# The first transfers, folds and sums of an autocorrelation and expert kernel on other queues and engines

## The reference, cut to what matters

```python
def _autocorrelation(Q, K, V):           # per batch, 8 heads, L = 512 positions
    qf = jnp.fft.fft(q, axis=2)
    kf = jnp.fft.fft(k, axis=2)
    corr = jnp.fft.ifft(qf * jnp.conj(kf), axis=2).real
    topk = int(C * np.log(L))            # 12
    w, idx = jax.lax.top_k(corr.transpose(0, 1, 3, 2), topk)
    w = jax.nn.softmax(w, axis=-1)
    for i in range(topk):
        g = jnp.minimum(idx[:, :, None, :, i] + pos, L - 1)
        out = out + w[:, :, None, :, i] * jnp.take_along_axis(v, g, axis=2)

x = x + jnp.tanh(g_xattn[0]) * _L0_xattn_ref(_layernorm(x), ctx_4096, ctx_4096)
x = x + jnp.tanh(g_ffn[0]) * _L0_ffn_ref(_layernorm(x), W_base, b_base, W_gate, W_thr, b_thr, A_w, B_w)
```

## Time and profile before

| | us |
|---|---|
| median of 3 runs | 3143.74 |
| lowest and highest | 3143.69 and 3145.4 |
| the profiled execution's own time | 3146.76 |
| its span, first to last instruction | 3145.0 |
| TensorE busy | 2976.3 (95%) |
| VectorE, GpSimd, ScalarE busy | 1699.9, 1494.1, 861.7 |

### The profile page before, as it was taken

How to read it: one execution, slowest core, us unless ns; L and a number is a source line. 1 busy time by engine, 2 the same in 40 slices (tenths; PEclk the granted TensorE clock), 3 DMA queues, 4 the chain that set the end, 5 groups by cost and what they waited for, 6 DMA issues and landing times.

```text
span 3145.0 us, 35465 instructions
## 1 busy us (share of the span) xinstructions
PE 2976.3 (95%) x12496; PEld 1510.2 (48%) x12496; DVE 1699.9 (54%) x2863; ACT 861.7 (27%) x1253; POOL 1494.1 (48%) x582
## 2 busy tenths in 40 slices
PE   4999999999999999999579999999999999999999
PEld 2545544554545455454354444444444444444444
DVE  4899999999999999988561121121121121121111
ACT  3343334334333433432251111121121121111110
POOL 4878887887888788886212211211211212212210
PEclk8999999999999999999799999999999999999999
DMA  9445544544454455341363232232232232232330
GB/s 213 120 117 127 133 105 120 133 115 113 124 140 101 119 132 119 86 99 49 134 228 86 76 107 82 78 107 78 82 107 75 85 107 72 88 107 67 93 94 28
DMA packets 268310, 333.59 MB, mean 106 GB/s; under 512 B 167321, under 2 KB 167449, under 8 KB 253497
## 3 DMA queue, kind: packets, MB, share of 16 engines
q1 hardware_dynamic: 268226, 332.68, 39.1%
HBM read 231.94 MB, written 67.11 MB: 95 GB/s over the span
## 4 chain that ended last, share of the span: by engine, by line
PE 46%; DVE 3%; DMA 1%; issue 1%; ACT 0%; POOL 0%; DVEq 0%; ACTq 0%; SPq 0%
PE bank L939 42%; DVE row L1094 2%; PE bank L928 1%; PE bank L929 1%; PE bank L930 1%; PE bank L919 1%; DMA row<-in_L_ffn_W_base_dram 1%; DMA row<-in_L_ffn_A_w_dram 0%; PE bank L956 0%; PE bank L954 0%; PE bank L955 0%; DVE w_lo L1033 0%; DMA nt<-wrow 0%; POOL wrow L1120 0%; PE bank L947 0%
## 5 line engine op out<-in xcount | busy, mean ns | idle before, releaser
L1120 POOL TENSOR_TENSOR wrow<-norm,wrow 128x2048 f16<-128x2048 f32 x32 | 130.3, 4071 | 1230.2 <-ACT wrow L992 1230.2
L720 POOL TENSOR_TENSOR spec_o<-spec_o,term 128x1024 f32<-128x1024 f32 x256 | 594.7, 2358 | 31.2 <-DVE term L558 31.2
L939 PE MATMUL bank<-w_hi,wrow 128*128 128x512 f16 x2048 | 489.3, 379 | 3.8 <-DVE row L1094 3.8
L939 PE MATMUL bank<-w_hi,nt 128*128 128x512 f16 x2048 | 489.0, 379 | 3.5 <-DVE row L1094 3.5
L381 PE MATMUL bank<-wt,table 128*128 128x512 f32 x1024 | 450.8, 598 | 25.8 <-DVE prod_b L535 19.0
L1087 DVE TENSOR_TENSOR hwt_lo<-bank,hwt_hi 128x128 f16<-128x128 f32 x32 | 9.3, 292 | 789.9 <-ACT hwt_hi L1011 789.9
L939 PEld LDWEIGHTS bank<-w_hi,wrow 128*128 128x128 f16 x2048 | 200.2, 98 | 251.7 <-DVE row L1094 13.7
L939 PEld LDWEIGHTS bank<-w_hi,nt 128*128 128x128 f16 x2048 | 200.6, 98 | 250.3 <-DVE row L1094 12.7
L381 PEld LDWEIGHTS bank<-wt,table 128*128 128x128 f32 x1024 | 193.1, 191 | 264.6 <-issue 235.7
L939 PE MATMUL bank<-w_lo,wrow 128*128 128x512 f16 x1024 | 262.8, 379 | 0.0
L939 PE MATMUL bank<-w_lo,nt 128*128 128x512 f16 x1024 | 262.8, 379 | 0.0
(11 more groups left out here) (153 smaller groups left out, 4449.4 us busy)
## 6 DMA issues: line engine op xcount, KB each, us to landing
xt<-in_x_dram SPq DMA_DIRECT2D x32, 1024.0 KB, 12.4
norm<-x_scratch SPq DMA_DIRECT2D x32, 1024.0 KB, 5.6
row<-x_scratch SPq DMA_DIRECT2D x32, 1024.0 KB, 7.0
out_dram<-row SPq DMA_DIRECT2D x32, 1024.0 KB, 4.4
xstat<-in_x_dram SPq DMA_DIRECT2D x28, 1024.0 KB, 10.5
vt<-in_ctx_dram SPq DMA_DIRECT2D x256, 64.0 KB
vt<-in_ctx_dram SPq DMA_DIRECT2D x64, 256.0 KB
xres<-in_x_dram SPq DMA_DIRECT2D x256, 64.0 KB
```

Source lines behind the costliest of these rows:

```text
L720: pool.tensor_tensor(to, to, term[:, buffer], sign).then_inc(term_added, 1)
L939: mm = pe.matmul(dense[o][:, :], nt(par, part)[:, k, :], w[:, k, o * 512:(o + 1) * 512], start=(k == 0 and n == 0), stop=False)
L1120: pool.tensor_tensor(norm_lo, norm[:, :], norm_hi, ALU.subtract).then_inc(norm_lo_made, 1)
```

## The change

It has five parts, all ahead of or in the first step. The first two chunks of x are loaded ahead of everything else. The ten transfers of the first v are issued by ScalarE instead of SP. The table is loaded in four parts, two of which (for v and for q) are awaited before the first spectra and two later. The first chunk of x is not loaded a second time into xt: the first normalisation reads it from the buffer prod_a. The first folds of q and the first sums are made by VectorE instead of GpSimd.

```diff
-                load_v(0)
-                load_v_last(0)
-                sp.dma_start(table[:, :], tables[:, 0:I_AT]).then_inc(table_loaded, 16)
                 for n in range(NCH):
-                    sp.dma_start(early[n], x_t[0, :, :, n * C:(n + 1) * C]).then_inc(early_loaded[n], 16)
-                load_x(0)
+                    load_early(n)
+                    if n == 1:
+                        load_v_last(0)
+                        load_table(V_AT, P_AT, first_tables_loaded)
+                        load_table(Q_AT, W_AT, first_tables_loaded)
+                load_table(W_AT, V_AT, table_loaded)
+                load_table(P_AT, I_AT, table_loaded)
...
-                pe.wait_ge(table_loaded, 16)
+                pe.wait_ge(first_tables_loaded, 32)
                 v_spectra(0, X(0))
                 pe.wait_ge(ident_loaded, 16)
+                pe.wait_ge(table_loaded, 32)
...
                 def normalise(i):
-                    act.wait_ge(x_loaded, 16 * (i + 1))
+                    if least(i) >= 1:
+                        act.wait_ge(x_loaded, 16 * i)
                     act.wait_ge(ln1_ready, i // NCH + 1)
                     for t in range(TT):
-                        act.activation(xt[:, t, :], xt[:, t, :], ACT.Identity, bias=ln1_bias[:, t:t + 1],
+                        act.activation(xt[:, t, :], (xt if least(i) >= 1 else early[0])[:, t, :], ACT.Identity, bias=ln1_bias[:, t:t + 1],
...
+                for n in range(8):
+                    act.dma_start(vt[16 * n:16 * n + 16, 0:2, :], v_after[0, 7 - n, :, :, 0:C]).then_inc(v_loaded, 16)
+                for h in range(2):
+                    act.dma_start(vt[:, 2 + h, :], v_before[0, :, :, h, 0:C]).then_inc(v_loaded, 16)
                 act.wait_ge(ei_scale_set, 2)
...
+                def first_fold():
+                    dve.wait_ge(x_normed, 4)
+                    dve.tensor_tensor(qf[:, 0:2, :], xt[:, 0:2, :], xt[:, 2:4, :], ALU.add).then_inc(q_folded, 1)
+                    dve.tensor_tensor(qf[:, 2:4, :], xt[:, 0:2, :], xt[:, 2:4, :], ALU.subtract).then_inc(q_folded, 1)
+
+                def first_sums():
+                    dve.wait_ge(q_used, 2)
+                    dve.tensor_tensor(prod_a[:, 0:2, :], prod_a[:, 0:2, :], prod_b[:, 0:2, :], ALU.add).then_inc(prod_made, 1)
+                    dve.tensor_tensor(prod_a[:, 2:4, :], prod_a[:, 2:4, :], prod_b[:, 2:4, :], ALU.subtract)\
+                       .then_inc(prod_made, 1)
...
                 scales(0)
+                first_fold()
                 dve.wait_ge(gates_ready, 2)
...
                 join_v(0)
-                fold_q(0)
                 fold_v(1)
...
-                    if most(i) < STEPS:
+                    if least(i) >= 1 and most(i) < STEPS:
                         sum_qk(i)
```

More of the change, by code:

```diff
@@ L168, in flamingo_kernel @@
             early = [prod_a[:, :, :], halves[:, :, :], corr[:, :, :], wt[:, :, :]]
-            table_loaded = sem("table_loaded")
+            table_loaded, first_tables_loaded = sem("table_loaded"), sem("first_tables_loaded")
             ei_scale_set = sem("ei_scale_set")
@@ L244, in load_x, with load_table, load_early @@
                     sp.dma_start(xt[:, :, :], x_t[b, :, :, ds(c, C)]).then_inc(x_loaded, 16)
+                def load_table(first, last, loaded):
+                    sp.dma_start(table[:, first:last], tables[:, first:last]).then_inc(loaded, 16)
+                def load_early(n):
+                    sp.dma_start(early[n], x_t[0, :, :, n * C:(n + 1) * C]).then_inc(early_loaded[n], 16)
                 def load_res(i, par):
@@ L652, in step @@
                         q_times_k(i, par, mine)
+                    if most(i) == 0:
+                        first_sums()
                     if least(i) >= 1:
```

## The result

| | before | changed |
|---|---|---|
| median, us | 3144.57 (6 runs beside the change) | 3158.7 (6 runs) |
| lowest and highest | 3142.57 and 3146.84 | 3154.37 and 3159.48 |
| the profiled execution | 3146.76 | 3158.3 |
| its span | 3145.0 | 3156.5 |

The ratio is 1.0041, 95% interval 1.0028 to 1.0054: slower, by 14.1 us between the medians and 11.5 between the two profiled spans. The forecast was 3141.2, a gain, with a chance of 0.02 for a loss of this size.

A forecast was written before the change was run, and what follows sets the result against it. TensorE bounds the loop, so only the prologue chain, with v's and x's chains equally long, could shift: 0.5 + 0 + 1.0 + 1.0 = 2.5 us off the 3145.0 span, 3142.5, by offset 3141.2; range 3134.5 to 3145.0.

The forecast's parts named there:

- I take 13.4, 1.0 later than now, near the lower end because of the idle share: Prologue: first v on ScalarE's queue lands at 13.4 us, as x fits into half idle DMA; root 0.6 us later.
- upper bound of 18.0: Latest landing of the first v, if two x loads (2.1 MB at 385 GB/s, 5.4 us) all go first.
- the second v at 34.0: Prologue: v of chunk 1 lands near 34.0 us instead of about 40.4; GpSimd folds it 34.0 to 38.7.
- the rule of two inputs: A VectorE instruction with two SBUF inputs and a GpSimd instruction reading SBUF share a port pair; the second fully blocks.
- First folds on VectorE, gain 0.5: Folds of q take 2.3 us for 4.65, but VectorE waits for GpSimd until 38.7; end 41.0 against 41.50.
- rival A: VectorE is free of GpSimd: 2.3 us for folds, 2.3 for sums, more in step 1; 8 us, 3135.5; chance 0.2.
- First sums, gain 0: Sums before the correlation: VectorE takes turns with GpSimd's folds of the second q; 2.3 if VectorE keeps its turn.
- Step 1, gain 1.0 + 1.0: Third v comes 2.8 us earlier, no longer late: 1.0 us; shorter TensorE idle before L381, clock effect: 1.0 us.
- The table in parts, nothing: Prologue: parts V and Q in by about 16 us, before v is ready: no effect; at 164 GB/s loses 1 us.
- So a gain can only be a shift: The change touches only what precedes the loop: later steps start earlier by the prologue's saving, nothing else gets cheaper.
- Rival B: x's queue is served first, v lands at 18.0, folds end 2.8 us later, step 1 returns 1.0: 3145.5; chance 0.1.
- the break-even landing of 16.2: First v landing after 16.2 us puts the folds' end at 42.5, taking back all that step 1 gives.

The follow-up runs named there:

- the fastest version: Kernel before with v first, folds and sums on VectorE, b_w later, GpSimd's second v and sixth statistics moved back, other reorderings: 3138.56 us, ratio 0.9981.

## Why the prediction was wrong

- **The step that failed: "I take 13.4, 1.0 later than now, near the lower end because of the idle share".** v landed at 21.56, 9.1 later than before and beyond the upper bound of 18.0. The bound let only x's first two chunks go first, 2.1 MB at 385 GB/s. The runs showed 4.0 MB of the other queue moved before v was there, and both together at 207 to 263 GB/s from 6 to 21 us; v's own queue had 27 to 79 GB/s, against 118 alone. (An estimate: 5.1 MB at 385 GB/s take 13 us and so would be there near 15. The bytes alone explain part of the delay, the low rate the rest.) The idle share of 0.52 was read as room for x without cost to v; x took it, and v paid. Behind the landing the chain went as written: root +8.7, right after the table load.
- The Trainium skill's rule ("DMA: Bandwidth & Descriptors", "Issuing engines are not separate DMA queues") was on the right side: the second queue saves only time of the issuing sequencer. That section says that the transfers run on the same engines and interleave, and names no rate. Here v got the smaller part of them, and the sum was about 40% below that of x alone, on two queues as on one (200 GB/s, above); no run shows why.
- **Missed: the refining instructions.** The collision of VectorE with GpSimd's folds of the second v was foreseen, but for the folds of q. The forecast had the second v at 34.0 (bounds 32.6 and 36.5), again by the idle start, and GpSimd through with it at 38.7. It came at 41.4, and its folds fell on the seven small instructions behind the root at 40.80. With v at 34.0 they would have been over even before this late root. Each small instruction that waits goes in a turn of its own, so two of 0.16 us cost as much as two large ones: +4.1. One of the two (L81) has one input in SBUF, so the rule of two inputs, as quoted in the prediction, does not cover it.
- *First folds on VectorE, gain 0.5*: measured 2.3, as in rival A, but only since no work of GpSimd met them. Where they did meet (x waiting for v) the pair took 5.5 us, a loss of 0.9. And on the kernel before 2.1 us at the folds were 0.8 at the correlation.
- *First sums, gain 0*: right. 4.5 us, one held up to 3.38 by fold_q(1). VectorE does not keep its turn. Rival A's 2.3 needs GpSimd to be held back.
- *Step 1, gain 1.0 + 1.0*: near in size, 1.3 together, but not for the reason given. The third v was to be loaded 2.8 us earlier; its issue came 8.4 us later (74.69 against 66.33), and it was in time only because the weights were 11.1 us later. That part is luck. GpSimd then waited for VectorE, and after a gap of 2.92 us the transform took 15.67 for 16.95; the granted clock is 0.50 still, in 101 to 103 us as in the earlier trace rows.
- *The table in parts, nothing*: the part for q landed at 21.5, not by 16, and that costs nothing in the changed kernel only since v is later still. With v first TensorE had to wait for it until 19.87, 1.5 us later than before, where the bound had 1.0.
- **Missed: the loop is not untouched.** "So a gain can only be a shift" left out that four more instructions on VectorE ahead of the loop can make one of its instructions late: 1.9 us.
- Rival B had the mechanism (v late, the loss taken at the root) and the break-even landing of 16.2; at its own landing of 18.0 it gave 3145.5, a loss of 1.8. By its arithmetic a landing of 21.5 gives a loss of 5.4; the profiled pair has 11.5, and the rest is the refining and the loop. A chance of 0.1, and a landing capped at 18.0, were too little: nothing in the trace before shows two queues at once, and the bound should have left the rate open.

The sum as measured in the profiled pair: v +8.7, refining +4.1, folds -2.3, sums and what follows +0.4, step 1 -1.3, loop +1.9: 11.5 us.

## What to carry to other kernels

A DMA engine that is half idle under one pattern of transfers is no free room: what fills it can slow the first transfers down. Move a load to a second queue only after a run has shown the landing times of both, and count the bytes of each queue. Look at what stands ahead of the critical instruction on its own engine: a load for later statistics hid the gain of the folds, and instructions of 0.16 us cost 4 us. On a chain with two inputs of equal length it is likely best to load first what has the longer compute chain behind it; the fastest version does, but with other edits. And a gain in a prologue is kept only if the next late thing (here a load behind the expert weights, then a statistics load) moves with it.

## What was not expected of the hardware

- Two queues together moved 207 to 263 GB/s at a busy share of 1.04 to 1.08; x alone 385 at 1.04. The queue with v had 27 to 79 GB/s of it, against 118 alone, and the 1 MB of v landed at 21.56 and not at 11.04. One queue with v behind x moved as little (200 GB/s at 1.08).
- VectorE and GpSimd take turns, instruction by instruction, where VectorE adds, multiplies or corrects two tensors in SBUF, also for instructions of 128x4 numbers, and for a TENSOR_SCALAR with one tensor input: 2.27 us for 0.17. VectorE's statistics (2.46 us at 27.20) and its products from PSUM (1.22 at 58.01) ran at their usual pace beside GpSimd's instructions.
- Four one-column memsets ahead of a loop made it 1.7 us longer in one kernel and 2.6 shorter in the other, through a delay of 0.35 us on one instruction in every fourth step.
